# Turning probabilities, normalised inputs and y by VectorE blocks and DRAM round trips instead of TensorE transposes, in a skewed attention and FFN kernel

## What is computed

```python
# x: 8 batches x 1024 rows x 256, float32; LN is a layer norm without weights
x = x + LN(attention(LN(x)))       # causal, q = xn@Wq, k = xn@Wk, v = xn@Wv, softmax(q k^T / 16) v @ Wo
x = x + LN(LN(x) @ W[idx] + b[idx])  # idx = argmax(log_softmax(logits) + gumbel(u)), one of 8 matrices
```

## Time and profile before

| | us |
|---|---|
| median of 3 runs | 425.56 |
| the runs | 426.36, 425.56, 425.23 |
| profiled execution: span, first to last instruction | 424.3 |
| TensorE busy / VectorE busy / ScalarE busy / GpSimd busy | 414.0 / 339.8 / 299.1 / 118.3 |

### The profile page before, as it was taken

The page is one execution under the profiler, slowest core; times in us unless marked ns, Lnnn a source line. Parts: engine busy times, 40 slices in busy tenths (PEclk is TensorE's granted clock), DMA queues, the critical chain, the costliest instruction groups (busy, mean ns, idle before and its releaser), DMA issues.

```text
span 424.3 us, 9812 instructions
## 1 busy us (share of the span) xinstructions
PE 414.0 (98%) x3045; PEld 393.2 (93%) x3045; DVE 339.8 (80%) x1010; ACT 299.1 (71%) x854; POOL 118.3 (28%) x237
## 2 busy tenths in 40 slices
PE   7999999999999999999999999999999999999993
PEld 7789999999999999999999999999999999999993
DVE  4578778987898878887788878898788887876776
ACT  5886877668766687568866687666885678756563
POOL 3103333232322232123421323223232224302133
PEclk9999999999999999999999999999999999999998
DMA  6310012110120101201021001201012000020003
GB/s 198 90 49 26 26 25 76 52 39 14 51 81 18 49 25 42 82 9 40 25 66 57 25 25 48 76 25 49 13 37 99 0 0 0 25 75 2 2 0 101
DMA packets 18951, 18.46 MB, mean 44 GB/s; under 512 B 1140, under 2 KB 18932, under 8 KB 18932
## 3 DMA queue, kind: packets, MB, share of 16 engines
q1 hardware_dynamic: 18660, 17.96, 13.5%
q10 hardware_dynamic: 272, 0.26, 0.2%
HBM read 9.83 MB, written 8.39 MB: 43 GB/s over the span
## 4 chain that ended last, share of the span: by engine, by line
PE 93%; DMA 2%; ACT 2%; DVE 1%; issue 0%; POOL 0%; SPq 0%; POOLq 0%; DVEq 0%
PE bank L805 54%; PE score L805 23%; PE bank L908 7%; PE bank L932 3%; PE bank L819 3%; DMA wq<-in_L_attn_Wq_dram 1%; DMA bias_raw<-in_L_ffn_b_dram 1%; PE score L891 1%; PE score L847 0%; PE bank L865 0%; POOL f_rstd L387 0%; PE score L835 0%; DVE out_sb L778 0%; ACT squares_junk L591 0%; ACT sums_junk L470 0%
## 5 line engine op out<-in xcount | busy, mean ns | idle before, releaser
L387 POOL TENSOR_TENSOR o_rstd<-o_ve,minus_half 128x1 f32<-128x1 f32 x64 | 35.2, 550 | 193.8 <-DVE o_ve L735 193.8
L805 PE MATMUL bank<-v_hi,pT_lo 128*128 128x256 f32 x288 | 84.6, 294 | 0.0
L805 PE MATMUL bank<-v_hi,pT_hi 128*128 128x256 f32 x288 | 81.4, 283 | 0.0
L805 PE MATMUL bank<-v_lo,pT_hi 128*128 128x256 f32 x288 | 81.3, 282 | 0.0
L805 PE MATMUL score<-xT_hi,g_lo 128*128 128x384 f32 (+4 forms) x176 | 63.7, 362 | 0.0
L805 PE MATMUL score<-xT_hi,g_hi 128*128 128x384 f32 (+4 forms) x176 | 61.1, 347 | 0.0
L805 PE MATMUL score<-xT_lo,g_hi 128*128 128x384 f32 (+4 forms) x176 | 61.1, 347 | 0.0
L549 ACT ACTIVATE probs<-neg_scores,neg_max 128x128 f32<-128x128 f32 (+3 forms) x64 | 49.7, 776 | 14.0 <-DVE neg_max L707 13.5
L805 PEld LDWEIGHTS bank<-v_lo,pT_hi 128*128 128x128 f32 x288 | 55.0, 191 | 0.4
L805 PEld LDWEIGHTS bank<-v_hi,pT_lo 128*128 128x128 f32 x288 | 54.9, 191 | 0.3
L805 PEld LDWEIGHTS bank<-v_hi,pT_hi 128*128 128x128 f32 x288 | 54.9, 191 | 0.0
(11 more groups left out here) (112 smaller groups left out, 1130.5 us busy)
## 6 DMA issues: line engine op xcount, KB each, us to landing
x_sb<-in_L_attn_x_dram SPq DMA_DIRECT2D x32, 256.0 KB, 2.7
out_dram<-out_sb SPq DMA_DIRECT2D x31, 256.0 KB, 2.1
wq<-in_L_attn_Wq_dram ACTq DMA_DIRECT2D x1, 256.0 KB, 4.1
wk<-in_L_attn_Wk_dram SPq DMA_DIRECT2D x1, 256.0 KB, 4.4
wv<-in_L_attn_Wv_dram SPq DMA_DIRECT2D x1, 256.0 KB, 4.2
wo_raw<-in_L_attn_Wo_dram SPq DMA_DIRECT2D x1, 256.0 KB, 4.5
wf_raw<-in_L_ffn_W_dram SPq DMA_DIRECT2D x1, 256.0 KB, 2.7
out_dram<-out_sb SPq DMA_DIRECT2D x2, 128.0 KB, 2.1
```

What stands on the lines that cost most here:

```text
L387: return nc.gpsimd.tensor_tensor(dst[:, n0:n1], ve[:, n0:n1], minus_half[:, n0:n1], ALU.pow)
L805: last = nc.tensor.matmul(dst, l, r, start=(i == 0), stop=(i == len(passes) - 1))
```

## The change

The three kinds of transposes leave TensorE, except in weight preparation, for batch 0's x, and at the end of batch 7 (T4 to T7 and the last y units).

A turn now goes so. VectorE transposes 32x32 blocks inside each 32 partitions, into `p_turn`, `x_turn` or `y_turn` (steps Q, B, I). SyncE writes the buffer to DRAM in one transfer (P, W, Y in its order), waits until that has landed, and fetches it back with four transfers, one for each 32 partitions, which moves the blocks to their places (Q, R, J). ScalarE rounds `hi` out of SBUF; `lo` is made on GpSimd for p and y (P and J in `POOL_ORDER`), and on VectorE, from SBUF, for x (X).

`yn` and its step K, `y_nm` and `y_shift` are gone: y itself is turned. F multiplies y with a `wf` that is centred over its input rows as well (once, with a matmul of a matrix of 1/256 and a VectorE subtraction), and VectorE scales by `y_rstd` while it adds the bias, tile by tile. Results go into `f_sb` itself.

The orders carry steps of other batches: a ' marks a step of the batch before, and L, H, B, X, G are of the one after. O6, O7, and all of F, U and Z of a batch run in the next round. A round of the loop has the same products as a batch before.

```diff
-    PE_ORDER = """S0 V0 S1 V1 T0 S2 T1 S3 O0 V2 T2 O1 S4 T3 V3 O2 S5 O3 T4 S6 T5 S7 X0 Y0 O4 T6 O5 T7 O6 X1 Y1
-        O7 F0 G0 Y2 X2 F1 X3 F2 Y3 G1 G2 F3 G3"""
+    PE_ORDER = """S0 S1 S2 S3 O6' O7' F0' V0 S4 S5 V1 O0 F1' S6 O1 S7 O2 O3 V2 F2' F3' V3 O4 O5 G0 G1 G2 G3"""
+    ACT_ORDER = """P7' G3' E0 E1 J1' E2 E3 H0 O6' H1 J2' O7' H2 F0' V0 P0 P1 E4 V1 E5 P2 O0 H3 J3' F1' P3 O1 E6 O2 E7 O3 V2
+        P4 P5 F2' F3' V3 X0 X1 O4 X2 X3 J0 O5 G0 G1 G2 P6"""
+    POOL_ORDER = """P6' P7' J1' L0 L1 N2' L2 C6' J2' C7' U0' P0 P1 N3' L3 P2 C0 J3' P3 C1 U1' C2 C3 P4 P5 U2' N0 C4 J0 C5
+        U3' N1"""
+    SP_ORDER = """J2' P0 P1 Q0 Q1 A3' Y3' Z0' J3' P2 W0 Q2 R0 A0 Y0 Z1' P3 A1 J0 Y1 Q3 J1 Z2' A2 Y2 Z3'"""
...
+            def fetch(raw, kept, loaded):
+                for q, source in enumerate(kept):
+                    sp.dma_start(raw[q * QUAD:(q + 1) * QUAD].rearrange("a (i r) -> a i r", i=QUADS), source
+                                 ).then_inc(loaded, 16)
...
+                    elif kind == "P":
+                        sp.wait_ge(p_turned, b.count(NT, 2 * n + 2))
+                        sp.dma_start(p_kept[n].rearrange("p q r -> p (q r)"), p_slot(n)).then_inc(p_written[n], 16)
+                    elif kind == "Q":
+                        sp.wait_ge(p_written[n], b.count(16, 16))
+                        fetch(p_slot(n), p_kept[n].rearrange("(i a) q r -> q a i r", i=QUADS), p_loaded[n])
...
+                        pool.wait_ge(p_hi_ready, b.count(NT, n + 1))
+                        nc.gpsimd.tensor_tensor(p_half(pT_lo, n), p_quads(n), p_half(pT_hi, n).bitcast(f32),
+                                                ALU.subtract).then_inc(p_lo_ready, 1)
...
+                        act.wait_ge(p_loaded[n // 2], b.count(QUADS * 16, QUADS * 16))
...
+                        nc.scalar.activation(p_half(pT_hi, n), p_quads(n), ACT.Identity).then_inc(p_hi_ready, 1)
...
+                        nc.vector.transpose(p_quads(n), probs[:, n % 2, 0:(n + 1) * PART].rearrange(
+                            "p (u q a) -> p u q a", q=QUADS, a=QUAD)).then_inc(p_turned, 1)
...
+                            last = nc.vector.scalar_tensor_tensor(out=f_sb[:, p, t % 2, :],
+                                                                  in0=bank[job.bank][:, (t - t0) * D:(t - t0 + 1) * D],
+                                                                  scalar=y_rstd[:, t:t + 1], in1=bias[:, :],
+                                                                  op0=ALU.mult, op1=ALU.add)
```

More of the change, by code:

```diff
@@ L73, in sandwich_block_kernel @@
[L73 to L81, removed]
@@ L110, in pieces, with __init__, count, index @@
         return (1, w) if w <= BANK else (2, w // 2)
-    def jobs_of(steps):
-        for kind, n in steps:
+    class Batch:
+        def __init__(self, s, ahead):
+            self.s, self.ahead = s, ahead
+            self.known = s + ahead if isinstance(s, int) else None
+            self.last = self.known == B - 1
+        def count(self, per, extra):
+            return self.s * per + (self.ahead * per + extra)
+        def index(self):
+            return self.s + self.ahead if self.ahead else self.s
+        def parity(self):
+            return (self.s + self.ahead % 2) % 2
+        def other(self, by):
+            return Batch(self.s, self.ahead + by)
+        def exists(self, first=0):
+            return self.known is None or first <= self.known < B
@@ L308, in cols, with raw_block, split_block, p_slot @@
             return bank[bk][:, 0:n]
+        def raw_block(c, k):
+            cols_of = x_turn[:, :].rearrange("p (i k t s) -> p k t i s", i=QUADS, k=KC, t=NT)
+            return cols_of[:, k, c * (NT // 2):(c + 1) * (NT // 2), :, :]
+        def split_block(half, c, k):
+            return half[:, k, c * BANK:(c + 1) * BANK].rearrange("p (t i s) -> p t i s", t=NT // 2, i=QUADS)
+        def p_slot(p):
+            at = sum(4 * q + 3 for q in range(p)) * PART
+            return p_turn[:, at:at + (4 * p + 3) * PART]
@@ L426, in _ @@
+            for p in range(NP):
+                x_scales(Batch(0, 0), p)
+            sequence(0, POOL_ORDER)
+            with pool.Fori(1, B - 1) as s:
+                sequence(s, POOL_ORDER)
+            sequence(B - 1, POOL_LAST)
         @block.scalar
@@ L635, in x_statistics, with x_blocks @@
                                         ALU.add).then_inc(x_ve_ready, 1)
+            def x_blocks(b, p):
+                dve.wait_ge(xn_ready, b.count(NP, p + 1))
+                if b.known != 1 and p == 0:
+                    dve.wait_ge(x_lo_ready, b.count(2 * KC, -2 * KC))
+                turned = x_turn[:, :].rearrange("p (q k t s) -> p t k q s", q=QUADS, k=KC, t=NT)
+                for t in (2 * p, 2 * p + 1):
+                    last = nc.vector.transpose(turned[:, t], xn[:, t, :].rearrange("p (k q a) -> p k q a", k=KC, q=QUADS))
+                last.then_inc(x_turned, 1)
             def copy_transposed(n):
```

602 lines of the change are left out of this document (379 added, 223 removed).

## The result

The changed kernel takes 434.33 us (median of 4 runs, 433.51 to 435.36) against 425.77 for the kernel before beside it: 1.0184 times as long, 95% interval 1.0144 to 1.0225. The forecast was 398.6, range 380 to 432, so both the side and the range missed. The span is 431.7 us, 34.4 more than the 397.3 of the sum.

The account below looks back on a forecast made before the run. VectorE was to replace TensorE as the bound, 46.5 us a round with one wait. Span 23.3 + 35 + 6 x 46.5 + 60 = 397.3, with 1.3 for the runs' median 398.6 us; range 380 to 432.

Parts of the forecast that it names:

- 42.3 us a round: TensorE's own work after losing 68 transposes of 0.1125 us, 7.65 us, from a round of 49.92.
- VectorE's sum: VectorE's round: 34.4 us left of its old work plus 10.7 for 24 block transposes, 45.1 us, the next bound.
- Hidden: GpSimd's added subtractions, taken at 15 us, make it busy 28 of 46 us a round, so they cost no time.
- rival 2: VectorE's two-SBUF-input instructions (X, Z) and GpSimd's subtractions lock each other out: 3.2 us a round, 417.8 us; chance 0.10.
- the sign it named: The lock between VectorE and GpSimd would show if Z (L1003) lengthened beyond 0.5 us.
- 45.1 + 1.4 = 46.5: Steady round in us: VectorE's work plus a wait of about 1.5 us behind the fetch of y.
- the one wait that it had walked: ScalarE's J0 waits for the fetch of y's pair 0, landing at about 39 where wanted at 37.5: about 1.5 us.
- rival 1: Transfers bind, as 32-partition fetches run at half of 313 GB/s: round 52.5 us, 434.6 us; chance 0.17.
- Its sign: Transfers binding would show if ScalarE's waits for p_turn, x_turn or y_turn summed to over 5 us a round.
- Rivals 3 to 5: Block transposes cost two passes (453 us, 0.08) or half (377.6, 0.10), or queue skew eats the gain (419 to 426, 0.05).
- Rival 5: In-order queues wait for each other as long as before, T = 49.9 to 51, 419 to 426 us; chance 0.05.
- Round 0 and batch 7: First round 35 us (31.4 of TensorE plus 3.6 for the late x fetch); last batch 60 us, 0.7 for waits.

Follow-up runs that it names:

- short turns: VectorE transposes only the first 128 columns of each tile, against the changed kernel: 425.03 us, round 49.72.
- J0 and no lock: Changed kernel with step J0 moved behind G2 and N1 and GpSimd's subtractions made one column and a fill: 415.87 us, round 48.11.
- Z last: Reordered kernel (five places, J0 later, one-column instructions) with Z3' also behind I2 and G2, last in VectorE's round: 416.97 us.
- J0's move: ScalarE's and GpSimd's step J0 put behind G2 and N1, against the changed kernel: 426.3 us, round 49.88.
- the fills: GpSimd subtracts one column and fills the rest with zeros: 426.55 us against the changed kernel's 434.3; 415.87 with J0 also later.
- small transfers: Each write and fetch moves only 32 of a quarter's columns, against the changed kernel: 432.61 us, round 50.77.
- the best version that leaves nothing out: Kernel with Z3' last in VectorE's round, plus loads A0, A1 behind Q3 and store Z1' behind P3 in SyncE's order: 412.8 us.
- the new order: Five places of ScalarE's and VectorE's orders changed, on top of J0 later and one-column instructions: 417.72 us; 402.6 with 32-column transfers.
- everything taken out: Changed kernel with J0 later, 32-column transfers, GpSimd fills for subtractions and 128 columns per block transpose: 391.06 us, round 44.66.

## Why the prediction was wrong

**TensorE.** Nearly right. 42.3 us a round were forecast; measured were 43.0 to 44.3 in rounds at a granted clock of 1.00, which is 2.4 GHz. What the sum left out is that the clock doesn't stay there once TensorE waits: the stretches at 1.2 GHz, shown above, bring four of the five settled rounds of the changed kernel to a mean of 0.97. These four took 50.7 to 51.4 us, the one at 1.00 took 50.6. With short turns the rounds go to and fro between 49.0 us at 1.00 and 50.1 at 0.93.

**VectorE's sum.** Right as a price of its work. The transposes' groups are busy for 12.2 us a round (for x and y 21.2 / 7 and 22.2 / 7.25, for p the sum of its eight forms, 6.1), less 16 overlaps of 0.08 us with a neighbour 10.9, against 10.7 in the sum; the 1024-column one 1.233 us against "near 1.2". Without the subtractions beside it (J0 and no lock) its work is 43.6 us, 1.5 under the 45.1. The busy time of 46.4 us comes near the sum only because this and the lock's 2.7 offset each other in part, which is luck.

**GpSimd.** Its price was right: 2.39 us for 1024 columns, 29.8 us in the round against 28. "Hidden" was not: it holds VectorE, and with Z last the chain that ends last runs over it.

**The lock (rival 2).** This is one of the two steps that failed: the sum let VectorE's steps pass GpSimd's new subtractions at no price. The rival was priced at 3.2 us, and 2.7 a batch were measured; the sign it named was met, Z at 515 ns. That the sizes are near is luck, for it named the wrong instructions. X kept its price (689 ns, where 693 was the row), since no subtraction of GpSimd ran where X stood, and Z was a small part at first; 19 of the 21.5 us were in the two-column instructions with a single input, which the sum had at no risk. And it was treated as a cost to add, with a chance of 0.10, though every batch before had only GpSimd instructions of one or two columns and the change put 15 us of long ones beside VectorE. The Trainium skill says both (SBUF — State Buffer, Who interferes with whom): two SBUF inputs exclude a GpSimd instruction that reads, and `tensor_scalar` in its two-port mode excludes any. I used the first half. The runs agree with both, down to the fill: it holds a two-column `y_ve` for its whole length (0.88 us beside a fill of 0.85) but leaves Z at 474 ns. What the lock costs in time is less sure than its size on VectorE. The 19 us of the two-column ones, taken away with the subtractions whole, bring 2.9 us alone and 0.7 beyond J0's move; the 7.8 and 10.4 us of the fills hold GpSimd's shorter steps as well.

**The sum "45.1 + 1.4 = 46.5".** This is the other step, and the larger. It took the one wait that it had walked (J0, 1.5 us; measured 3.2 on ScalarE, 2.2 on VectorE) for all there would be. Measured idle time of VectorE was 4.2 us. Of the 4.1 us by which the steady round of 50.6 exceeds 46.5, 2.8 are this and 1.3 are VectorE's busy time. The pieces can't all be added up from single edits: J0's place 8 us, the fills for subtractions 8 alone and 10 beyond J0, the small transfers from a loss of 9 to a gain of 15 us by what else is there. What can be said is what the round is in an order that fits: 45.7 us with the small transfers, and 47.4 in the best version that leaves nothing out. So a good part of the miss was the order's; that the whole kernel can reach the forecast's 46.5 is not shown, and its best time, 412.8 us, is 14 above the forecast.

**Transfers (rival 1).** Its side and nearly its time came out (434.6 against 434.3). The time is luck: the rival had rounds of 52.5 us, measured were 50.7, and round 0 and batch 7 made up the rest. Its sign was met: ScalarE's waits for `p_turn`, `y_turn` and `x_turn` are 20.9 + 19.1 + 0.8 us in the run, 5.8 a round. But the sign was a poor one: it counted waits on an engine that had 18 us to spare. Its mechanism came out in part. The mean is far above the 216 GB/s that the rival needed: 82.21 MB in 66.0% of the span, 288 GB/s at full use against 313 before. The mean hides two rates. These are the stretches from the landing of x's first fetch to that of its last, from there to the landing of P3's write, and from the first landing of that fetch, Q3, to its last (columns as above):

```profile
254.92:258.52 3.60, 2.52 (x21) 2.52 (x22) 3.49 (x13) 2.77 (x10) 3.19 (x2) 1.00 1.08 231
258.52:262.68 4.16, 4.16 (x33) 3.94 (x32) 3.58 (x10) 3.05 (x9) 2.04 (x3) 1.00 1.04 406
266.48:269.76 3.28, 1.76 (x9) 1.54 (x10) 3.13 (x11) 1.14 (x3) 2.10 (x4) 1.00 1.13 221
```

With the DMA engines busy all through, the core moved 231 and 221 GB/s while the fetches of 32 partitions landed, 1.1 to 1.2 us apart for 240 or 256 KB each, and 406 in between, where no fetch landed and writes and loads of 128 partitions did. The other rounds show the same (222 to 248, and 377 to 411). That the four fetches stand in the queue together was a reason given against the rival, and it doesn't hold in full: together they still ran at some 225 GB/s, not at half of 313, but well below it. Writes were faster than the sum had them, which is why the mean came out near. No run parts the 32 partitions from other causes, such as direction or the size of the pieces. The bound of the Trainium skill for one transfer to 32 partitions (SBUF — State Buffer, Door 1: The DMA port swizzle) was not tried by itself in these runs. What was missed most was the length of single trips: 8.3 us (median) for the write of 960 KB, which shares the engines with a fetch of 1 MB, and ScalarE's P6 starts 50.6 us after its round's S0 (218.69 against 168.13), where the walk had it landed by 45. That this length costs time, once the lock is out of its way, is shown by the 15 us of the small transfers in the new order.

**Rivals 3 to 5.** Transposes did not take two passes, nor half. Rival 5 (419 to 426, the in-order queues wait as long as before) had the kind of cause that was found, and a chance of 0.05.

**Round 0 and batch 7.** 42.7 against 35. TensorE is busy 36.0 us there instead of 31.4, at a mean granted clock of 0.92 (0.50 from 51.13 to 57.95), and it waits 4.4 us in one place, for R3, which V3 needs, behind VectorE's steps for batch 1 (TensorE's timeline):

```profile
51.88 0.58 PE L1027 MATMUL bank<-wvo_hi,xT_lo 128*128 128x256 f32 x1 [4.43 <-DVE y L956]
```

The sum had priced the fetch of x as what is late there (3.6 us); ScalarE's wait for x is 0.8 us in the whole run. No experiment was made on round 0 alone; by its M0s it is 44.3 us in the changed kernel, 39.6 with the new order and small transfers, and 36.6 with everything taken out. Batch 7 took 61.85 against 60.

## What to carry to other kernels

A busy sum per engine gives the round only if the order lets it be reached: when five in-order queues hand work round a loop, walk the whole loop, trips and queue places included, before adding one wait to the longest sum. Moving long two-input work to GpSimd has a price that its own busy time doesn't show, paid by whichever VectorE instructions happen to stand beside it; look for them among the small ones too. Removing one cost at a time can show nothing, or even a loss, where it pushes work into another cost, as the small transfers did here; try them in pairs before calling either harmless. And look at what else an experiment changes: a fill for a subtraction takes the lock away and more than half of the instruction's own time as well.
